# Decoder layer on one core: routing moved within the attention loop, row copies by transfer, bias and list scatters split and moved

## The reference

```python
x = _layernorm(x + _L0_attn_ref(x, ...))            # a recurrent mixer
x = _layernorm(x + _L0_xattn_ref(x, ctx_768, ...))  # cross-attention, 8 heads of 64
x = _layernorm(x + _L0_ffn_ref(x, ...))             # mixture of experts
```

```python
xn = _l2norm(xf)
group_scores = xn @ _l2norm(group_centroids).T      # 8 groups, the best 4 stay
expert_scores = xn @ _l2norm(expert_centroids).T + bias
top_scores, top_idx = jax.lax.top_k(masked, K)      # 32 experts, K = 4
gates = jax.nn.softmax(top_scores, axis=-1)
pos = jnp.cumsum(onehot, axis=0)[...] - 1           # place in the expert's list
keep = pos < capacity                               # 1280 places
```

## Time and profile before

| | us |
|---|---|
| median of 3 runs | 2309.27 (2308.49 to 2314.07) |
| the profiled execution, its own time | 2315.64 |
| its span | 2313.9 |
| PE busy | 2037.1 (88%) |
| DVE busy | 1604.8 (69%) |
| POOL busy | 1553.1 (67%) |
| ACT busy | 1217.5 (53%) |
| attention stage, loop over the groups, about | 326 to 1024 |
| end of the attention stage, to POOL's last instruction | 1024 to 1105 |

### The profile page before, as it was taken

How to read it: one execution, slowest core, us unless ns; L and a number is a source line. 1 busy time by engine, 2 the same in 40 slices (tenths; PEclk the granted TensorE clock), 3 DMA queues, 4 the chain that set the end, 5 groups by cost and what they waited for, 6 DMA issues and landing times. The chain is left out here.

```text
span 2313.9 us, 51923 instructions
## 1 busy us (share of the span) xinstructions
PE 2037.1 (88%) x14104; PEld 1779.5 (77%) x14104; DVE 1604.8 (69%) x3687; ACT 1217.5 (53%) x3390; POOL 1553.1 (67%) x1691
## 2 busy tenths in 40 slices
PE   5999689989899989951599999999999998299998
PEld 3555378777677767841599999999999998278887
DVE  4666547778777887752477778878677777157776
ACT  2555346545454555530477777777677776133332
POOL 3666503566665666676488888888788888257675
PEclk9999899999998998975799999999999999599999
DMA  4200012311231113110576776777677776334452
GB/s 130 82 0 0 14 54 69 98 56 55 65 99 55 55 55 102 53 55 1 165 235 228 231 236 225 239 233 229 224 230 231 234 234 218 127 144 165 172 194 106
DMA packets 238983, 312.37 MB, mean 135 GB/s; under 512 B 49546, under 2 KB 165170, under 8 KB 238932
## 3 DMA queue, kind: packets, MB, share of 16 engines
q1 hardware_dynamic: 212884, 262.67, 35.4%
q0 software_dynamic: 26048, 49.10, 5.8%
HBM read 236.17 MB, written 75.60 MB: 135 GB/s over the span
## 5 line engine op out<-in xcount | busy, mean ns | idle before, releaser
L1038 POOL DMA_INDIRECT slot_token<-a_entry,a_slot_i x256 | 258.7, 1011 | 158.9 <-issue 72.5
L1474 POOL DMA_INDIRECT part_rows<-e_out,e_dest x184 | 234.2, 1273 | 71.9 <-issue 64.1
L1466 POOL DMA_INDIRECT e_xg<-x_rows,e_tok x188 | 209.8, 1116 | 71.8 <-issue 56.1
L1607 ACT ACTIVATE e_sg<-e_g 128x256 f32<-128x256 f32 x368 | 141.7, 385 | 204.1 <-PE e_g L1303 186.6
L1656 DVE TENSOR_TENSOR e_h<-e_sg,e_u 128x256 f32<-128x256 f32 x368 | 157.7, 429 | 101.8 <-PE e_u L1303 50.8
L897 ACT ACTIVATE a_prob<-a_s,a_ntop 128x128 f32<-128x128 f32 x512 | 180.7, 398 | 0.7 <-DVE a_ntop L1239 0.7
L1671 DVE TENSOR_SCALAR e_out<-e_d,e_dest 128x256 f32<-128x256 f32 x184 | 80.6, 479 | 120.0 <-PE e_d L1303 120.0
L1482 POOL TENSOR_TENSOR e_wd0l<-e_raw_d,e_wd0h 128x256 fp32r<-128x256 f32 x184 | 139.2, 793 | 11.4 <-ACT e_wd0h L1587 10.6
L1482 POOL TENSOR_TENSOR e_wd1l<-e_raw_d,e_wd1h 128x256 fp32r<-128x256 f32 x184 | 138.3, 790 | 12.2 <-ACT e_wd1h L1587 11.4
L1886 ACT ACTIVATE f_sg<-f_g 128x512 f32<-128x512 f32 x64 | 38.3, 599 | 176.2 <-PE f_g L1303 176.2
L1303 PE MATMUL e_d<-e_wd1h,e_ht1h 128*128 128x256 f32 x368 | 108.5, 295 | 24.5 <-issue 24.5
(11 more groups left out here) (300 smaller groups left out, 7695.1 us busy)
## 6 DMA issues: line engine op xcount, KB each, us to landing
e_raw_g<-in_eg SPq DMA_DIRECT2D x94, 512.0 KB
e_raw_u<-in_eu SPq DMA_DIRECT2D x94, 512.0 KB
e_raw_d<-in_ed SPq DMA_DIRECT2D x93, 512.0 KB
part_rows<-a_zero SPq DMA_DIRECT2D x16, 2048.0 KB
f_part<-part_rows SPq DMA_DIRECT2D x16, 2048.0 KB, 9.5
x<-in_x SPq DMA_DIRECT2D x16, 512.0 KB, 3.4
x_rows<-x SPq DMA_DIRECT2D x16, 512.0 KB
f_xs<-x_rows SPq DMA_DIRECT2D x16, 512.0 KB, 4.7
```

Source lines behind the costliest of these rows:

```text
L1038: pool.indirect_dma_start(k.slot_tok, bass.IndirectOffsetOnAxis(ap=slot_i[:, j, q:q + 1], axis=0), entry[:, j, q, :], None, bounds_check=S ...
L1466: pool.indirect_dma_start(xg[a][:, n, :], None, k.x2_d, bass.IndirectOffsetOnAxis(ap=tok[a][:, n, 0:1], axis=0))\
L1474: pool.indirect_dma_start(k.part_d, bass.IndirectOffsetOnAxis(ap=dest[a][:, n, 1:2], axis=0), out[a][:, n, :], None).then_inc(put[a], 16)
L1607: act.activation(sg[m % 2][:], bank_g[m % 2][:, 0:SETW], ACT.Silu).then_inc(sg_rdy, 1)
```

## The change

- Copies of rows: `xs` and `rxs` are no longer copied by POOL (L964, L1001) but by transfers on SP's queue from SBUF to SBUF. PE's `t` and `rt` wait for the transfers (`xs_in`, `rxs_in`). PE transposes group 0 from x itself. SP's turn begins with `copy_rows(g+2)`, and `store` issues the copy to `rxs` ahead of the write of the rows.
- Bias: `biased(g+1)`, four instructions of 256 columns instead of one of 1024 for group g+2, behind `norms` in POOL's round; `finish` waits for its block's piece alone.
- Routing half a group sooner: FILL has rp in block 0 (ahead of q2), rt at the head of block 2 and rs after it; the banks of q2, q3 and of k0 to k2 are exchanged. `choose_groups` runs at the end of block 2, `choose_experts` in block 3 of the same group, `place` in block 1 of the next; `gate_exp` in block 0.
- POOL's round: `counted(g-2)` first; only batch 3 of a group's scatters is left for the next round, behind the context; batches 0 to 2 stand at the end, batch 1 behind the transposes and batch 2 behind the weighing of block 2, batch 3 behind the transposes of block 0.
- The end of the stage follows the new order.

```diff
-        FILL = [[[("t", 0, 0), ("t", 1, 1)], [("q", 0, 0), ("q", 1, 1)], [("q", 2, 0)]],
-                [[("q", 3, 1)], [("k", 0, 0), ("k", 1, 1)], [("k", 2, 0)]],
-                [[("k", 3, 1), ("rp", 0, 0)], [("rt", 0, 0), ("rt", 1, 1)], [("v", 0, 1), ("rs", 0, 0)]],
+        FILL = [[[("t", 0, 0), ("t", 1, 1)], [("q", 0, 0), ("q", 1, 1)], [("rp", 0, 0), ("q", 2, 1)]],
+                [[("q", 3, 0)], [("k", 0, 1), ("k", 1, 0)], [("k", 2, 1)]],
+                [[("rt", 0, 0), ("rt", 1, 1)], [("rs", 0, 0), ("k", 3, 1)], [("v", 0, 1)]],
                 [[("v", 1, 1)], [("v", 2, 0), ("v", 3, 1)], []]]
...
+                def copy_rows(g):
+                    for i in range(2):
+                        sp.wait_ge(a_done[i], ONE + before(g - 1, i) + upto(g - 1, "t", i))
+                        apart(sp, k.past_sp)
+                    sp.dma_start(xs[:], grouped(rows(k.x, g))).then_inc(xs_in, 16)
+
+                copy_rows(1)
...
                     sp.wait_ge(x2_rdy, ONE + g + 1)
+                    apart(sp, k.past_sp)
+                    if not isinstance(g, int) or g:
+                        for i in range(2):
+                            sp.wait_ge(a_done[i], ONE + before(g + 1, i) + upto(g + 1, "rt", i))
+                            apart(sp, k.past_sp)
+                    sp.dma_start(rxs[:], grouped(rows(k.x, g))).then_inc(rxs_in, 16)
                     sp.dma_start(k.x2_d[bass.ds(g * GW, GW), :].rearrange("(b t) d -> t b d", b=TG),
...
                         g = 2 * i + par
+                        copy_rows(g + 2)
...
                         if kind == "t":
-                            pe.wait_ge(xs_rdy, ONE + g + 1)
+                            first = isinstance(g, int) and g == 0
+                            if not first:
+                                pe.wait_ge(xs_in, DMA + 16 * g)
...
                         elif kind == "rt":
-                            pe.wait_ge(rxs_rdy, ONE + g - 2 + 1)
+                            pe.wait_ge(rxs_in, DMA + 16 * (g - 2 + 1))
...
-                def stage(g):
-                    pool.tensor_copy(xs[:], grouped(rows(k.x, g))).then_inc(xs_rdy, 1)
-                    pool.tensor_tensor(grouped(rows(k.x, g)), grouped(rows(k.x, g)),
-                                       k.bout[:, None, :].to_broadcast([P, TG, D]), ALU.add).then_inc(xb_rdy, 1)
+                def biased(g):
...
+                        pool.wait_ge(xs_in, DMA + 16 * g)
+                    for j in range(TG):
+                        pool.tensor_tensor(rows(k.x, g, j, 1), rows(k.x, g, j, 1), k.bout[:], ALU.add).then_inc(xb_rdy, 1)
...
-                    pool.tensor_copy(rxs[:], grouped(rows(k.x, g))).then_inc(rxs_rdy, 1)
...
-                        elif paced and j < 3:
-                            pool.wait_ge(v_done, ONE + TG * (r + 2) + 3 + j)
+                        elif paced and j == 1:
+                            pool.wait_ge(t_done, ONE + 2 * (TG * (r + 2) + 3))
+                        elif paced and j == 2:
+                            pool.wait_ge(v_done, ONE + TG * (r + 2) + 3)
                         elif paced:
-                            pool.wait_ge(t_done, ONE + 2 * (TG * (r + 3) + 2))
+                            pool.wait_ge(t_done, ONE + 2 * (TG * (r + 3) + 1))
...
                 def around(g):
-                        stage(g + 2)
+                    if after or g >= 2:
+                        counted(g - 2)
                     if after or g >= 1:
                         rstd(g - 1, not after and g == 1)
                     if after or g + 1 < NG:
                         context_low(g + 1)
                     if after or g >= 3:
-                        scatter(g - 3, (2,), after or g < NG)
-                    if after or g >= 2:
-                        counted(g - 2)
+                        scatter(g - 3, (3,), after or g < NG)
                     if after or g >= 1:
                         norms(g - 1, not after and g == 1)
-                    if after or g >= 3:
-                        scatter(g - 3, (3,), after or g < NG)
+                    if after or g + 1 < NG:
+                        biased(g + 1)
                     if after or g >= 2:
-                        scatter(g - 2, (0, 1), after or g < NG)
+                        scatter(g - 2, (0, 1, 2), after or g < NG)
...
-                scatter(NG - 2, (2, 3), False)
                 counted(NG - 1)
+                scatter(NG - 2, (3,), False)
                 scatter(NG - 1, range(TG), False)
...
                     if b == 3 and (not isinstance(g, int) or g >= 1):
-                        choose_groups(g - 1)
-                    if b == 0 and (not isinstance(g, int) or g >= 2):
-                        choose_experts(g - 2)
-                    if b == 2 and (not isinstance(g, int) or g >= 2):
+                        choose_experts(g - 1)
+                    if b == 1 and (not isinstance(g, int) or g >= 2):
                         place(g - 2)
...
                     emptied(g + 1, 1 - par, b, 2)
+                    if b == 2 and (not isinstance(g, int) or g >= 1):
+                        choose_groups(g - 1)
```

More of the change, by code:

```diff
@@ L656, in upto, with ended @@
             return same.index(job) + 1
+        def ended(g, kind):
+            return [(i, before(g, i) + max(upto(g, kind, m) for k_, m, j in whole(g) if (k_, j) == (kind, i)))
+                    for i in range(2)]
         def with_context(weights, cols, tokens):
@@ L742, in fill @@
                         if kind == "t":
-                            pe.wait_ge(xs_rdy, ONE + g + 1)
+                            first = isinstance(g, int) and g == 0
+                            if not first:
+                                pe.wait_ge(xs_in, DMA + 16 * g)
                             for j in range(TG):
-                                last = pe.transpose(out[:, j * P:(j + 1) * P], xs[:, j, m * P:(m + 1) * P], k.ident[:])
+                                row = rows(k.x, 0, j, 1) if first else xs[:, j, :]
+                                last = pe.transpose(out[:, j * P:(j + 1) * P], row[:, m * P:(m + 1) * P], k.ident[:])
                         elif kind == "q":
@@ L785, in scores @@
                     if b == 0:
-                        pe.wait_ge(a_out[0], ONE + before(g, 0) + upto(g, "k", 2))
-                        pe.wait_ge(a_out[1], ONE + before(g, 1) + upto(g, "k", 3))
+                        for i, count in ended(g, "k"):
+                            pe.wait_ge(a_out[i], ONE + count)
                     pe.wait_ge(e_rdy, ONE + s)
@@ L924, in slot @@
                         context_high(g + 1)
+                    if b == 0 and (not isinstance(g, int) or g >= 2):
+                        gate_exp(g - 2)
                     emptied(g + 1, 1 - par, b, 1)
@@ L961, in _ @@
                 pool.wait_ge(half_rdy, 1)
[L963 to L966 removed]
+                def biased(g):
+                    if isinstance(g, int) and g == 0:
+                        for i in range(2):
+                            pool.wait_ge(a_done[i], ONE + upto(0, "t", i))
+                    else:
+                        pool.wait_ge(xs_in, DMA + 16 * g)
+                    for j in range(TG):
+                        pool.tensor_tensor(rows(k.x, g, j, 1), rows(k.x, g, j, 1), k.bout[:], ALU.add).then_inc(xb_rdy, 1)
                 def context_low(g):
@@ L995, in norms @@
                     pool.tensor_tensor(nrm[:], dvrr[:], r_half[:], ALU.pow).then_inc(nrm_rdy, 1)
-                    pool.wait_ge(x2_rdy, ONE + g + 1)
-                    if not first:
-                        for i in range(2):
-                            pool.wait_ge(a_done[i], ONE + before(g + 1, i) + upto(g + 1, "rt", i))
-                        apart(pool, k.past_pool)
-                    pool.tensor_copy(rxs[:], grouped(rows(k.x, g))).then_inc(rxs_rdy, 1)
                 def counted(r):
@@ L1051, in around @@
                     after = not isinstance(g, int)
-                    if after or g + 2 < NG:
-                        for i in range(2):
-                            pool.wait_ge(a_done[i], ONE + before(g + 1, i) + upto(g + 1, "t", i))
-                        apart(pool, k.past_pool)
-                        stage(g + 2)
+                    if after or g >= 2:
+                        counted(g - 2)
                     if after or g >= 1:
```

24 lines of the change are left out of this document (9 added, 15 removed).

## The result

The changed kernel takes 2336.27 us, the median of 7 runs (2322.52 to 2348.23), beside 2309.14 for the kernel before in the same call: a ratio of 1.0111 with a 95% interval of 1.0073 to 1.015: a small loss, but outside the noise. My 2220.5 us and my range up to 2256 were wrong in sign.

The account below looks back on a forecast made before the run. PE was the engine to follow, limited by waits for DVE and ACT and the clock falling behind them. Saving 71.8 us in eleven groups plus 17 at the stage's end gave 2309.3 - 88.8 = 2220.5 us, range 2200 to 2256.

Parts of the forecast that it names:

- The stall is POOL's 3.45 us of copy and bias, standing on DVE: Block 0 of each group: POOL's copy and bias hold DVE, so PE's q products wait 3.8 us a group.
- floor of 39.1: Attention loop: the 40.3 us group at 389.2 less its waits for q and rxt, about 1.2 us.
- The rxt wait: PE's v product (L763) waits for ACT's copy of rxt, 1.0 us a group; rt's earlier slot should remove it.
- The pieces, cost nothing: Bias in four pieces of about 0.6 us behind the norms, near block 2's start: no cost to DVE.
- rival A: Bias pieces act as one 2.4 us hold on DVE; groups cost 43 us, total 2248 us; chance 0.20.
- The transfers on SP's queue, cost nothing: Two added 512 KB copies a turn land before PE needs them, rxs with 2.5 us slack: no cost.
- End of the stage, 17 us (12 to 20): Attention stage's end: POOL has six fewer scatters, earlier counting and less waiting, saving about 17 us.
- POOL's own round: POOL's work per group, 16.4 us of it scatters, comes to about 35.5 us and fits into 40.
- C: Rival: rp waits for POOL's count behind three scatter batches, holding PE; at 8 us wait 2327 us; chance 0.04.
- B: Rival: only the stage's end gains, as rp in block 0 still waits for DVE's q0 copy; 2288 us; chance 0.08.
- Fill order, routing and slots, cost nothing: Loop: same instructions in other slots, with ACT's bank copies just in time, 0 to 0.1 us.
- the sum: Whole kernel: 71.8 us from eleven groups at 40.5 us plus 17 at the stage's end, 89 us saved.

Follow-up runs that it names:

- E2: Kernel before with only the two row copies by transfers and the bias in four pieces behind the norms: 2234.0 us, ratio 0.968.
- E8: E2 with the bias as one instruction of 2.4 us at the head of the round: 2285.9 us, ratio 0.987.
- E10: E2 with the bias as one instruction, left behind the norms: 2249.9 us, ratio 0.968.
- E5: Changed kernel with the scatter order and gates of the kernel before, counted still first: 2252.5 us, ratio 0.973.
- E6: E2 with the gates of batches 1 and 2 away, so twelve scatters in a row: 2359.9 us, ratio 1.020.
- E7: Changed kernel with two bias pieces (1.4 us) between each two scatter batches at the end of the round: 2247.3 us, ratio 0.970.
- E3: Kernel before with the gate of scatter batch 1 gone, so eight scatters in a row: 2325.4 us, ratio 1.006.
- E4: Changed kernel with the gate of scatter batch 2 one block later, for runs of eight: 2281.4 us, ratio 0.987.
- E1: Changed kernel with the third scatter batch moved back behind the context, meant as runs of four: 2267.3 us, ratio 0.981.
- E14: E7 with one bias piece (0.7 us) instead of two between the batches, two ahead of them: 2269.7 us, ratio 0.987 to 0.981 as tabled: 0.981.

## Why the prediction was wrong, step by step

- **"The stall is POOL's 3.45 us of copy and bias, standing on DVE"**: right. E2 takes the copies off POOL and moves and cuts the bias, and leaves the order of all else; the group falls from 47.0 to 40.4, at a granted clock of 0.99 instead of 0.92; I had said 40.5, with a floor of 39.1. Nine of its groups lie at 39.4 to 40.3. The rxt wait goes too (0.4 us in all), without the new fill order that I had given the credit.
- **The pieces, cost nothing, rival A as bound**: right, but for the place, not for the cutting. E8 shows rival A's hold at the head of the round (I priced it at 43 a group, E8 measured 44.5); E10 shows that behind the norms even the whole instruction costs 0.3 to 0.7 us a group.
- **The transfers on SP's queue, cost nothing**: right. PE shows no wait for xs or rxs in the eleven groups of either kernel.
- **End of the stage, 17 us (12 to 20)**: right, 14.8.
- **POOL's own round**: this step failed. I counted the scatters as 16.4 us of POOL's time, asked only whether the round fits into 40 us, and costed their new place at nothing. The round did fit: in the changed kernel's eleven groups POOL waited 105 us for DVE. But three batches without a wait that holds are one run of twelve, and such a run costs 7 to 10 us a group (changed less E5: 7.0; E6 less E2: 10.1). What each of them holds up, and what I had put at nothing, is PE's semaphore updates. The changed gates were meant to keep the batches apart; POOL reaches them late, since batch 0 waits its turn behind batch 3, its landing, the norms and the bias pieces, and by then they are open.
- **The rivals**: C had the right suspect, POOL's three batches, and the right sign, with the wrong mechanism and a chance of 0.04. It looked for who waits for POOL. PE's wait for the count costs 1.3 us a group in E5, none in the changed loop. B and A were not what happened.
- **Fill order, routing and slots, cost nothing**: off by 1.2 us a group (E5's 41.6 less E2's 40.4), of the size of PE's wait for the count, for 7 us won at the end; on balance no gain (0.973 and 0.968).

One reading was incomplete. My remark for rival A, that DVE's held instruction at 717.33 had started first and was held nevertheless, leaves out what POOL did then. A scatter had started 0.40 us ahead of it, and POOL went from that into the copy without a gap, so these rows don't tell who wins between the two:

```profile
716.93 0.98 POOL L1038 DMA_INDIRECT slot_token<-a_entry,a_slot_i  x1 [0.30 <-issue]
```

E5 and E7 are the change with its runs cut into fours: their ratios of 0.973 and 0.970 give 2247 and 2240 us of 2309, inside my range and 26 and 20 over the forecast. With E2's groups and the changed kernel's end together the sum would be met (2235 less 15), but no run had both.

Why PE's updates come late in a run of indirect transfers is open. That they do is shown by E3, E4, E6 and the pauses. A statement of the Trainium skill (DMA: Bandwidth & Descriptors, Why a DMA increments its semaphore by 16 and not by 1) bears on it: for a transfer that POOL issues, all 16 DMA engines each post their own increment, whatever its shape. By that a run of twelve would post an estimated 192 semaphore writes. The trace agrees on the number: from 502.5 to 520.0 POOL's queue has 192 packets of 4 bytes beside 192 of 96 bytes. They leave on time, as shown above, so if they are the cause it is not by a backlog of their own; no run here separates them from the data or the descriptors, so they stay a candidate, and the number of increments wasn't varied.

## What to carry to other kernels

Treat a run of small indirect transfers as a load on TensorE's semaphore updates, not only as time on the engine that issues it: here runs of four with gaps of 1.7 us and more between them (E2) cost little, and in runs cut into fours a gap of 1.6 us helped much more reliably than one of 0.9. When DVE or ACT wait for "remote" on a single core, compare the end of the matmul they need with their start. A gate spaces them only if the engine arrives before it opens; look in the timeline whether it waited there. And when one edit of a bundle (here the copies and the place of the bias) carries the gain, measure it alone before the schedule around it is moved.

## What the runs showed of the hardware

- Twelve indirect transfers of 128 entries each, 1.28 us from start to start, delayed what waited for PE by 9 to 10 us (507.65 to 516.83, 509.56 to 519.70). Only PE's updates came late. The first late one belongs to a matmul that ended 1.4 to 5.1 us into the run (changed kernel), and the last stood 1.9 to 2.2 us behind the run's end. DVE's waits on "remote" in eleven groups: 0.0, 3.3 and 22.5 us with runs of four (E8, before, E5), 8.4 with runs of four and one of seven (E2), 47.6 with runs of eight in nine groups (E1), 109 with runs of twelve (E6).
- PE itself slows in such a run: 24.1 us of "issue" waits before L787 in the changed kernel's eleven groups against 4.1 in E2.
- In all sixteen profiles one batch of the loop stops behind its first scatter, for 2.93 or 2.94 us in fourteen of them (before: 748.9, changed: 744.2, E2: 696.7), for 5.6 in E7 and 3.9 in E14, where bias pieces stand near. It is the 113th scatter of the program each time, whatever the schedule and the time. The cause is open.
- A POOL instruction of 2.4 us that reads SBUF held short DVE instructions, a subtraction or comparison of two SBUF tiles as well as a cast or a scalar operation on one of 16 columns: on average 0.24 became 1.15 us (E10), some 0.2 became 1.99 (E8). In E10 ten of the eleven took 1.15 to 1.26, and each ended 0.03 or 0.04 us behind POOL's instruction.
